# Router matrix made inside tile 0's first chain, contexts 1 to 3 in halves, first quantisation by VectorE, and new instruction orders in a fused attention and expert kernel on one Trainium2 core

## What is computed

```python
x = x + fake_quant(LN(x)) @ fake_quant(ctx)      # 8 bit: round(v / s + z), clipped
q, k, v = h @ wq.T + bq, h @ wk.T + bk, h @ wv.T + bv      # h = LN(x)
x = x + attention(q, k, v)                       # of each token, over its 32 heads of 16
scores = (h @ Wq.T) @ keys.T                     # h = LN(x); 64 experts, best 16 by softmax
x = x + ((h @ A.T) * gate) @ B.T * 2
```

## Time and profile before

| | us |
|---|---|
| median of 3 runs | 146.35 |
| lowest, highest | 144.74, 147.44 |
| the profiled execution | 145.24 |
| its span, first to last instruction | 143.2 |
| granted TensorE clock, mean | 0.988 |

### The profile page before, as it was taken

The page is one execution under the profiler, slowest core; times in us unless marked ns, Lnnn a source line. Parts: engine busy times, 40 slices in busy tenths (PEclk is TensorE's granted clock), DMA queues, the critical chain, the costliest instruction groups (busy, mean ns, idle before and its releaser), DMA issues.

```text
span 143.2 us, 4290 instructions
## 1 busy us (share of the span) xinstructions
PE 118.7 (83%) x1860; PEld 70.1 (49%) x1860; DVE 96.8 (68%) x195; ACT 69.2 (48%) x88; POOL 47.5 (33%) x61
## 2 busy tenths in 40 slices
PE   0029559999597999895989999997999899899992
PEld 0023344455546538463555453963644367374881
DVE  5847975046987998695773167889245958995522
ACT  0366930997389994232847694328210124611120
POOL 3018204186727915722016787000207200002000
PEclk9999986999999999999999999999999999999999
DMA  2899999999999400059992100000001000000102
GB/s 58 304 416 419 387 432 390 409 398 387 413 426 389 181 5 0 5 199 389 370 422 96 73 7 0 5 5 0 5 16 60 0 5 5 0 5 0 73 0 73
DMA packets 7380, 24.43 MB, mean 171 GB/s; under 512 B 1217, under 2 KB 1473, under 8 KB 5698
## 3 DMA queue, kind: packets, MB, share of 16 engines
q1 hardware_dynamic: 7216, 24.16, 43.3%
q10 hardware_dynamic: 146, 0.01, 0.1%
HBM read 23.11 MB, written 1.05 MB: 169 GB/s over the span
## 4 chain that ended last, share of the span: by engine, by line
PE 55%; DVE 17%; ACT 8%; issue 7%; DMA 7%; POOL 3%; SPq 1%; DVEq 0%; ACTq 0%; POOLq 0%
PE ps_b L1173 18%; PE ps_a L1173 11%; DMA raw<-in_ctx_dram 7%; PE ps_att L1255 5%; ACT cu L467 3%; PE ps_att L1318 3%; DVE cu L687 3%; PE ps_att L1266 2%; PE ps L1108 2%; PE ps_t L1154 2%; PE ps_t L1127 2%; PE ps L1241 2%; DVE qT L794 1%; DVE eT L820 1%; ACT v_diag L493 1%
## 5 line engine op out<-in xcount | busy, mean ns | idle before, releaser
L374 POOL TENSOR_SCALAR cbf<-cu 128x2048 bf16<-128x2048 uint8 x13 | 24.9, 1923 | 15.9 <-ACT cu L467 9.7
L467 ACT ACTIVATE cu<-raw,sc_in,sc_recip 128x2048 uint8<-128x2048 f32 x13 | 26.9, 2090 | 3.0 <-DMA raw<-in_ctx_dram 2.9
L352 POOL TENSOR_SCALAR var_eps<-mean_var 128x1 f32<-128x1 f32 x11 | 3.0, 268 | 44.0 <-DVE mean_var L644 44.0
L1255 PE MATMUL ps_att<-kT,qT 16*32 16x32 f32 x1024 | 10.7, 193 | 3.9 <-issue 2.3
L1255 PEld LDWEIGHTS ps_att<-kT,qT 16*32 16x32 f32 x1024 | 9.6, 104 | 7.6 <-issue 7.5
L493 ACT COPY v_diag<-vT 32x512 f32<-32x512 f32 x16 | 10.1, 633 | 2.4 <-DVE vT L802 2.1
L642 DVE BATCH_NORM_STATS2 stats<-x_sb 128x6 f32<-128x512 f32 x12 | 8.1, 679 | 3.6 <-POOL x_sb L391 3.5
L1108 PE MATMUL ps<-q1T,cbf 128*128 128x33 bf16 x256 | 8.4, 178 | 2.6 <-DVE cbf L705 1.2
L1108 PEld LDWEIGHTS ps<-q1T,cbf 128*128 128x128 bf16 x256 | 7.6, 96 | 5.4 <-issue 2.3
L1085 PE MATMUL ps_t<-ident_bf,q 128*128 128x128 bf16 x16 | 1.8, 245 | 9.8 <-DVE q L672 9.8
L387 POOL TENSOR_TENSOR attn<-oT,o_recip 128x512 f32<-128x512 f32 x3 | 4.0, 1339 | 15.6 <-DVE o_recip L830 15.6
(11 more groups left out here) (148 smaller groups left out, 236.1 us busy)
## 6 DMA issues: line engine op xcount, KB each, us to landing
raw<-in_ctx_dram SPq DMA_DIRECT2D x13, 1024.0 KB, 10.6
raw<-in_ctx_dram SPq DMA_DIRECT2D x6, 512.0 KB, 11.3
wq<-in_L_attn_wq_dram SPq DMA_DIRECT2D x1, 1024.0 KB, 13.6
wk<-in_L_attn_wk_dram SPq DMA_DIRECT2D x1, 1024.0 KB, 13.4
wv<-in_L_attn_wv_dram SPq DMA_DIRECT2D x1, 1024.0 KB, 15.7
wa<-in_L_ffn_A_w_dram SPq DMA_DIRECT2D x1, 1024.0 KB, 12.8
wb<-in_L_ffn_B_w_dram SPq DMA_DIRECT2D x1, 1024.0 KB, 11.0
out_dram<-x_sb SPq DMA_DIRECT2D x3, 256.0 KB, 2.0
```

The costliest lines, as they stand in the source:

```text
L374: nc.gpsimd.tensor_scalar(cbf[:, n % BF_SLOTS, :, :], cu8[:, n % U8_SLOTS, :], -CENTER, 1.0, ALU.add, ALU.mult).then_inc(sem_ctx_bf_pool, 1)
L467: nc.scalar.activation(cu8[:, n % U8_SLOTS, :], raw[:, n % RAW_SLOTS, :], ACT.Identity, bias=sc_in[:, 3:4], scale=sc_recip[:, 2:3]).then_i ...
L1255: last = nc.tensor.matmul(ps_att[Q * j:Q * j + H, i, :], qT[rows, i, :], kT[rows, i, :], start=True, stop=True)
```

## The change

It has six parts.

1. **Contexts 1 to 3 in halves.** Context 1 now is loaded in two transfers; ACT quantises its first half and DVE its second (`quantise_ctx_half`). Context 2 passes from DVE to ACT, in halves. Context 3 stays in halves.
2. **x by DVE.** Tile 0's `quantise_x` passes from ACT to DVE (`quantise_first_x`).
3. **The router's matrix early.** Its two loads go from behind context 7 to right behind context 3, ahead of `wq`. The transposes stand before `transpose_y1(0)`, the combination (now into `ps_att`) before `transpose_h2(0)`, the two ACT copies before `copy_first_h2T`.
4. **Loads reordered.** `x` of tile 1 goes behind `wq`; `x` of tiles 2 and 3 goes ahead of context 7.
5. **Dummies.** `keep_busy` has 128 columns in place of 512; there are 3 before product 3 of tile 0, 2 before and 3 behind the combination. `keep_clock_up(5)` is removed.
6. **Orders redone** on all engines.

```diff
-        halved = (BPT - 1, 2 * BPT - 1)
+        halved = (1, BPT - 2, BPT - 1, 2 * BPT - 1)
 # SP
             load_ctx(3)
+            sp.dma_start(wr[:, :, :], chunked(wrT)).then_inc(sem_router_in, 16)
+            sp.dma_start(keys[:, :], keysT).then_inc(sem_router_in, 16)
+            sp.dma_start(wq[:, :, :], chunked(wqT)).then_inc(sem_wq_in, 16)
             load_x(1, 2, sem_x1_in)
-            sp.dma_start(wq[:, :, :], chunked(wqT)).then_inc(sem_wq_in, 16)
...
+            load_x(2, 4, sem_x_rest_in)
             load_ctx(7)
-            load_x(2, 4, sem_x_rest_in)
-            sp.dma_start(wr[:, :, :], chunked(wrT)).then_inc(sem_router_in, 16)
-            sp.dma_start(keys[:, :], keysT).then_inc(sem_router_in, 16)
 # ACT
-            quantise_x(0)
             quantise_ctx(0)
             quantise_ctx(1)
+            quantise_ctx(2)
             quantise_ctx(3)
...
             shift_x(0)
+            copy_router_rows()
+            copy_router_weights()
             copy_first_h2T()
+            quantise_x(1)
             quantise_ctx(4)
-            quantise_x(1)
             quantise_ctx(5)
+            quantise_ctx(6)
             copy_q1T(1)
+            quantise_ctx(7)
             shift_x(1)
-            quantise_ctx(6)
-            quantise_ctx(7)
             quantise_ctx(8)
-            copy_router_rows()
+            quantise_ctx(9)
+            exp_scores(0, 0)
             quantise_x(2)
-            quantise_ctx(9)
             copy_h2T(1)
-            copy_router_weights()
             quantise_ctx(10)
-            exp_scores(0, 0)
             exp_scores(0, 1)
             copy_q1T(2)
+            quantise_ctx(11)
             place_v(0)
-            quantise_ctx(11)
 # DVE
             norm_1(0)
+            quantise_first_x()
             center_q1(0)
...
-            quantise_ctx(2)
+            quantise_ctx_half(1)
             center_ctx(2)
             center_ctx(3)
...
             bias_q(0)
+            spread_heads(qT, q_sb, sem_q_biased, sem_qT_ready, 0)
             bias_k(0)
-            spread_heads(qT, q_sb, sem_q_biased, sem_qT_ready, 0)
...
+            transpose_probs(1, 1)
             choose_experts(0)
-            transpose_probs(1, 1)
 # PE
             product(0, 2, 3)
+            keep_busy(3)
             product(0, 3, 4)
+            transpose_router_weights()
             transpose_y1(0)
+            keep_busy(2)
+            combine_router_weights()
             keep_busy(3)
             transpose_h2(0)
...
             product(1, 0, 1)
-            project_v(0, first)
             product(1, 1, 2)
             product(1, 2, 3)
             scores(0, 0)
+            project_v(0, first)
             product(1, 3, 4)
-            transpose_router_weights()
             transpose_y1(1)
+            scores(0, 1)
             project_v(0, second)
-            combine_router_weights()
             transpose_h2(1)
-            scores(0, 1)
-            transpose_q1(2)
             project_q(1, first)
             project_q(1, second)
+            transpose_q1(2)
             project_k(1, first)
             project_k(1, second)
+            product(2, 0, 1)
             context(0)
-            product(2, 0, 1)
...
             transpose_zg(2)
-            keep_clock_up(5)
             output(2, first)
```

More of the change, by code:

```diff
@@ L365, in center_ctx @@
                                             ALU.add, ALU.mult).then_inc(sem_half_bf_pool, 1)
-                    pool.wait_ge(*quantised(n))
+                    for landed in quantised(n):
+                        pool.wait_ge(*landed)
                     pool.wait_ge(sem_half_bf_pool, 1)
@@ L618, in _ @@
             apply_norm_3(1)
+            shift_x(3)
+            copy_q1T(3)
             copy_h3T(1)
+            place_v(2)
+            exp_gates(1)
             exp_scores(2, 0)
-            exp_gates(1)
-            place_v(2)
+            copy_zgT(1)
             exp_scores(2, 1)
-            copy_zgT(1)
             apply_norm_2(3)
@@ L679, in copy_q1T, with quantise_first_x, quantise_ctx_half @@
                 nc.vector.tensor_copy(q1T[:, t, :, :, 0:L], src).then_inc(sem_q1T_ready, 1)
-            def quantise_ctx(n):
+            def quantise_first_x():
                 dve.wait_ge(sem_recip, 1)
-                for half in range(2):
-                    part = slice(HALF * half, HALF * (half + 1))
-                    dve.wait_ge((sem_vector_half_in, ctx_in[n])[half], 16)
-                    nc.vector.tensor_scalar(cu8[:, n, part], raw[:, n, part], sc_recip[:, 2:3], sc_in[:, 3:4],
-                                            ALU.mult, ALU.add).then_inc(sem_ctx_u8_vector, 1)
+                dve.wait_ge(sem_ln1_done, 1)
+                nc.vector.tensor_scalar(h1_u8[:, 0, :], h1[:, 0, :], sc_recip[:, 0:1], sc_in[:, 1:2],
+                                        ALU.mult, ALU.add).then_inc(sem_x_u8, 1)
+            def quantise_ctx_half(n):
+                dve.wait_ge(sem_recip, 1)
+                dve.wait_ge(ctx_in[n], 16)
+                nc.vector.tensor_scalar(cu8[:, n, HALF:], raw[:, n, HALF:], sc_recip[:, 2:3], sc_in[:, 3:4],
+                                        ALU.mult, ALU.add).then_inc(sem_ctx_u8_vector, 1)
             def center_ctx(n):
@@ L693, in center_ctx @@
                 if n == BPT - 1:
-                    dve.wait_ge(sem_half_u8, 1)
+                    dve.wait_ge(*first_half_quantised(n))
                     nc.vector.tensor_scalar(cbf[:, n, 0:KC // 2, :], cu8[:, n, 0:HALF], CENTER, None,
                                             ALU.subtract).then_inc(sem_half_bf, 1)
-                    dve.wait_ge(*quantised(n))
+                    for landed in quantised(n):
+                        dve.wait_ge(*landed)
                     dve.wait_ge(sem_half_bf, 1)
@@ L1027, in _ @@
             bias_v(2)
+            transpose_v(2)
             softmax_shift(2, 0)
-            transpose_v(2)
             finish_product(3)
             choose_experts(1)
-            transpose_probs(2, 0)
             softmax_shift(2, 1)
+            residual_1(3)
             gates(1)
-            residual_1(3)
             gate_z(1)
             norm_2_stats(3)
+            transpose_probs(2, 0)
+            transpose_probs(2, 1)
+            transpose_context(2)
             sum_gates(1)
-            transpose_probs(2, 1)
             residual_3(1)
-            transpose_context(2)
+            norm_3(2)
             bias_q(3)
             spread_heads(qT, q_sb, sem_q_biased, sem_qT_ready, 3)
-            norm_3(2)
             bias_k(3)
@@ L1230, in combine_router_weights @@
                 pe.wait_ge(sem_wr_rows, 1)
[L1231 removed]
+                pe.wait_ge(sem_bias_spread, 3)
                 for c in range(KC):
[L1233 to L1234 removed]
+                    last = nc.tensor.matmul(ps_att[:, c * E // H:(c + 1) * E // H, :].rearrange("p i h -> p (i h)"),
+                                            wr_rows[:, c * P:(c + 1) * P], keys[:, :], start=True, stop=True)
                 last.then_inc(sem_wr_keys_done, 1)
@@ L1378, in _ @@
             project_q(2, first)
-            transpose_q1(3)
             project_q(2, second)
             project_k(2, first)
-            product(3, 0, 1)
             project_k(2, second)
+            transpose_q1(3)
             project_v(2, first)
@@ L1386, in _ @@
             scores(2, 0)
+            product(3, 0, 1)
+            transpose_h3(1)
             product(3, 1, 2)
-            transpose_h3(1)
             product(3, 2, 3)
```

70 lines of the change are left out of this document (33 added, 37 removed).

## The result

| | before | after |
|---|---|---|
| four executions each, median (span of values) | 146.89 (144.74 to 148.94) | 147.41 (146.42 to 148.59) |
| the profiled execution, and its span | 145.24, 143.2 | 147.83, 145.4 |
| a later, larger sample (36 and 12 executions) | 145.48 (143.32 to 148.99) | 146.79 (144.60 to 148.34) |

The ratio was 1.0186, with an interval of 1.0119 to 1.0253; in the larger sample 1.0082, 1.0013 to 1.0152. A ratio leaves out executions more than 1.5% above the fastest of their kernel, so it can differ from that of the medians. The changed kernel is slower, by 1 or 2%, where I had forecast no change. The 147.4 lies inside the range given.

A forecast was written before the change was run, and what follows sets the result against it. PE's dense part and its waits set the end, with loads a second bound until 47 us. Terms -0.1 + 1.1 - 0.4 - 0.2 - 0.4 - 0.1 = -0.1 took the median from 146.35 to 146.3; range 142.6 to 148.8.

The forecast's parts named there:

- the sentence on the clock: Tile 0's projections: PE's waits of some 5 us between 27 and 46 us make a lower clock free up to 2.8 us.
- The fourth product of tile 0: PE, tile 0: starts at 17.75 in place of 18.58, 0.8 us less, with context 2 off DVE.
- The transposes of h2: PE, tile 0: start at 22.5 to 23.8 against 24.82, 1.0 to 2.3 us earlier, taken as 1.8.
- the new wait that the prediction gave DVE: DVE, tile 0: free at 19.4, waits for x of tile 1, landing at 19.0 plus up to 1.5 us.
- Tile 1's fourth product: PE, tile 1: context 7 lands at 37.35, 1.65 us later, so this product starts at 39.75 against 39.09.
- the two chains: Up to `project_q(1)`: context 7's path gives 46.8, ACT's 46.5, against 46.90; of 1.8 us early, 0.1 is left.
- the second chain: ACT, tile 1: contexts 8 and 9, an exp and an x precede the h2T copy, giving 46.5 for `project_q(1)`.
- The wait before `context(0)`: PE waits 1.25 us for v, placed by ACT behind context 11; 1.1 us lost, between nothing and 1.4.
- PE's stalls go: Rival, tile 1's scores: stalls of 2.3 us fall elsewhere, 144.0, or a new one of 1.5 arises, 147.8; chance 0.13.
- small gains: Behind `context(0)`: 0.4 before `context(1)`, 0.2 before h3(2), 0.4 from the last tile's dummies, 0.1 from tile 1's gates.
- The small transfers ahead of the contexts: Rival, load queue: the router's 64-byte rows delay contexts, costing 1 to 4 us, 147.3 to 150.3; chance 0.17.
- The early gain: Rival, tile 0 to the end: the early 1.8 us survive and `context(0)`'s wait may shrink, 143.0; chance 0.25.

The follow-up runs named there:

- e5: Changed kernel with its eight narrow dummies replaced by seven of 512 columns, five of them in PE's waits between 27 and 42 us; 143.94 us, ratio 0.9954.
- e6: Changed kernel with x of tiles 2 and 3 loaded behind context 7 again; 146.23 us, ratio 1.0080.
- e7: Changed kernel with no edit, measured again beside the kernel before; 146.79 us, ratio 1.0082.
- e2: Changed kernel with tile 2's q1 transposes ahead of the second query projection and v placed ahead of context 11, as before; 147.64 us, ratio 1.0206.
- e10: e5 with `keep_clock_up(5)`, the last tile's dummies ahead of the third output projection, put back; 145.74 us, ratio 1.0110.
- e8: Kernel before with q of tile 0 spread before k's bias is added and the last tile's five dummies removed; 143.97 us, ratio 0.9925.
- e1: Changed kernel with 18 more narrow dummies in PE's waits between 27 and 42 us; 155.45 us, ratio 1.0671.
- e11: e5 with its five wide dummies in tile 1's stage replaced by twenty narrow ones at the same places; 160.45 us, ratio 1.1128.
- e12: e8 with one wide dummy ahead of `product(1, 3, 4)` and one ahead of `transpose_h2(1)`; 143.84 us, ratio 0.9911.

## Why the prediction was wrong

**The step that failed** is the sentence on the clock: "PE now waits some 5 us in all between 27 and 46 us, so a lower clock in tile 0's projections costs nothing up to 2.8 us." It took PE's new waits as cover for a lower clock. But the low clock comes with such waits: with them filled it is absent (e5), with them there it came in most executions, though not in all (e6, e7). And it looked for the low clock in tile 0's projections, where PE has room; it came at 35.6 to 49.3 us, in the stage that leads to `project_q(1)`. Term of the sum: -0.1 forecast for the start of `project_q(1)`, +3.4 measured in the profiled execution, -0.2 with the waits filled (e5: 46.69). What I could have seen: the lower clock of the earlier trace rows stood behind a stretch in which PE waited for contexts, and my own chain put the same kind of stretch ahead of tile 1. That it must fall there no row could tell: behind the 1.62 us wait of the earlier trace rows it had stayed at 1.00. It was a case that wanted a price and a chance, and had neither.

**Right, once the clock is taken out.** The fourth product of tile 0 (17.75, measured 17.73). The transposes of h2, "22.5 to 23.8", a little better at 22.36. x of tile 1 was there when DVE came to it at 19.29, so the new wait that the prediction gave DVE stayed away. Tile 1's fourth product, forecast at 39.75 from the order of the loads, is at 39.59 in e5 (40.55 with the low clock), and ACT quantised context 7's second half at 37.26 in the changed kernel, after 37 us as forecast. `project_q(1)`, 46.8, is at 46.69. So 2.5 us of early start in tile 0 were worth 0.2, as the two chains said. In e6 the second chain held the h2T copy, together with DVE's wait for x.

**The wait before `context(0)`**: 1.25 forecast; 1.28 and 1.29 measured. Its loss on the path, 1.1, was 1.3. That it is not ACT's order but ACT's amount of work (e2) I hadn't said.

**Stalls of PE.** I expected those of the earlier trace rows to stay. They went: 2.3 us before, none after. It is the rival "PE's stalls go", with 0.13, and nothing in the sum foresaw it: without this luck the changed kernel would be slower still, and the 147.4 owes its place inside the range to it. The sum, corrected term by term: -0.1 forecast, +3.5 for `project_q(1)`, +0.2 for the wait at `context(0)`, -2.6 for the stretch with the stalls (4.7 behind at the products of tile 2, 2.1 at h3 of tile 0; the stalls are 2.3 of it), and +1.2 for the small gains below make +2.2; the last matmul is 2.3 behind.

**Small gains.** I had forecast 1.1 us of gain in all; from h3 of tile 0 to the last matmul (2.12 behind, 2.26 behind) a loss of 0.1 came. The 0.42 us before `context(1)` did go (2.1 behind became 1.6), but PE then stood 0.87 us before `output(0)`, where it stood 0.24 before (2.4 behind). The row names the copy of zgT, which had ended at 76.14, 0.46 us before the matmul; e10 stood 1.44 us at this place with no releaser. So I take it for a stall like those in the scores, which is argued and not shown. The 0.68 before h3 of tile 2 went too, and `scores(3, 0)` right behind waited 0.73 us for kT, as the prediction said; 0.1 was kept, where 0.2 was forecast, since kT itself came 2.4 us later than before. For the last tile's dummies 0.4 us were forecast: from the transposes of zg to the last h3 the changed kernel took 4.76 us and the kernel before 5.05, 0.3 less, as between e5 and e10, where the dummies alone differ. `context(3)` ahead of it ran for 1.41 us in place of 1.16 and took that back.

**The other rivals.** The small transfers ahead of the contexts held up nothing: e5 meets the forecast that has no price for them, and the rate was 361 GB/s in the fifth slice and above 385 in the eight behind it, against 387 and above before. The price of that rival rested on the spread of context 7's halves (2.4 us against 1.3), which has another reading: they were issued 4.3 us apart, those of context 3 0.8. So the sign of that rival (slower) came true through another mechanism, which shouldn't count for it. The early gain wasn't kept.

**Open.** Device time stood 2.1 us above the span in the kernel before (median of 36) and 2.6 in the changed one (of 12), 1.8 in e5. The trace doesn't show what lies there; 0.5 us of the loss is in it. Why PE stands without a releaser in some kernels and not in others was priced, not explained. Nor do the runs show why the same waits bring the clock down in one execution and not in another. The kernel before has one profile; whether its stalls of 2.3 us stand in every execution isn't known, and the gain of e8 hangs on that.

## What to carry to other kernels

A wait that an earlier start opens in front of a dense stage is not free cover: look at what the granted clock does behind the nearest such wait, and price the dense stage at the lower level as a case of its own. If a filler is needed, let it be few wide matmuls and not many narrow ones, and put it in the wait ahead of the stage that counts. And where a change takes a short wait away, look at the next matmuls behind it: three times here the wait stood again within two operations (e2, e6, and the 0.68 us before h3 of tile 2). A wait marked as without a releaser is worth a look at the other engines' rows: that of 0.73 us here was for kT.

## What the runs showed of the hardware

PE was idle for 0.84, 1.40 and 0.54 us between 27 and 35 us, and the granted clock was 0.50 (1.2 GHz) from 35.6 to 49.3 us, through stretches in which PE was busy for 4.00 of 4.00 us. With these waits filled it stayed at 1.00 (e5). With 0.76, 1.41 and 0.54 us it also stayed at 1.00 in e6's profile, and in e7's, with 0.82, 1.42 and 0.54, until 41 us. The price was four passes of 512 columns in 3.78 us in place of 1.96, twice. The same kernel varies from execution to execution in when and how long it is low (mean clock 0.952 to 0.988 in the changed one), and the spread of 3.7 us in its times goes with it: 144.60 to 145.17 at 0.986 and above, 147.81 and 148.34 at 0.952 and 0.953.

PE stood without a releaser, mostly in groups of many small matmuls: 2.3 us in the kernel before, none in the changed one and in e8 (the 0.87 us before `output(0)` apart), 0.4 in e5, 6.0 in e1 (18 narrow dummies added), 8.9 in e11 (the wait of 0.7 us for kT is left out). In e12 1.39 us of it stood among eight matmuls of 512 columns. Going from five wide to twenty narrow dummies of nearly equal column time cost 16.5 us in device time. What PE waits for then the profile doesn't show.
